# Attention of layer 1: the upper half copy of a slot's keys goes from VectorE to ScalarE

## The chip, the cores and the metric

The kernel runs on one core of one Trainium2 chip. The metric is the time of one execution on the device in microseconds, as the median of several runs.

## What is computed

The network has two layers, each an attention block and a feed-forward block, with a layer norm ahead of each and a residual behind it. The input is 16 sequences of 512 tokens with 256 features. Here only the attention block of layer 1 matters:

```python
h = _layernorm(x, ln1_g, ln1_b)
q, k, v = heads(h @ WQ + bQ), heads(h @ WK + bK), heads(h @ WV + bV)   # 16 heads of 16
scores = einsum('bhqd,bhkd->bhqk', q, k) / sqrt(16)
allowed = (diff >= 0) & (diff < 128)                   # each token sees the last 128
attn = softmax(where(allowed, scores, -inf))
attn_out = (attn @ v) @ WO + bO
u = h @ Bw;  s = A * s + u_t (scan over tokens);  ssm_out = states @ Cw
g = sigmoid(h @ Wg + bg)
x1 = x + g * attn_out + (1.0 - g) * ssm_out
return x1 + gelu(_layernorm(x1) @ W1 + b1) @ W2 + b2   # the MLP, 1024 wide
```

## The kernel before

The program is four phases, one after the other: attention 0 (names a_), a mixture of experts (b_), attention 1 (c_, `attn1_phase`), and a second mixture (d_). Each engine has its own instruction list, and semaphores tie the lists together. What is told here is of `attn1_phase`.

**One sequence at a time.** Each engine runs a `body(it)` for the 16 sequences, written out one after the other. In a body stand first the attention steps of sequence it, then, interleaved, the output part and the MLP of sequence it and the projections of sequence it+1. So the MLP of one sequence and the preparation of the next share the engines, in an order that is written out by hand. The profile's queues hold to that order: an instruction that waits holds up all that stand behind it on its engine.

**Slots.** The 16 heads go in 8 pairs, called slots here (j = 0 to 7). Queries and keys are projected in a packed form. `spread_qk` (TensorE, L2021) multiplies them by a table that lays the two heads of a slot out over 128 partitions: the first head on partitions 0 to 63, the second on 64 to 127. It has four matmuls a slot, two for the queries into one PSUM bank and two for the keys into another, each 128x512. Then the copies: ScalarE's `q4_copy` (L1638) takes the queries' bank to SBUF as a whole. VectorE's `k4_copy` takes the keys' bank to SBUF in two half copies of 64x512: the lower half (L1818) into `k4[0:64, j, 0]`, the upper half (L1819) into `k4[64:128, j, 1]`. The other quarters of `k4` are zeros, so that one matmul gives the scores of both heads. The semaphore `k4_ready` goes up once a slot.

**Banks.** Slots 0 to 2 (HELD = 3) use the banks `o_ps` for the queries and `c_ps` for the keys, slots 3 to 7 the two banks of `ab_ps`. There is one bank for queries and one for keys, so the matmuls of slot j wait until slot j−1 is copied: the queries' for `q4_ready`, the keys' for `k4_ready`.

**Where the slots stand.** Slots 0 to 2 of the next sequence stand in the MLP of this one: slot 0 before the first block of `mlp1`, slot 1 after its second block, slot 2 before the last block of `mlp2`. Slot 3 opens the body, and slots 4 to 7 follow the scores of steps 0 to 3.

**Steps.** 32 steps a sequence (n = 0 to 31): four blocks of 128 queries, eight slots each. A step is: scores on TensorE (`scores`, L2047 and L2048, into one of two banks `s_ps`), their maxima on VectorE (`maxima`, L1839), exponentials with their sums on ScalarE (`exp`, L1658, two a step), reciprocals of the sums on VectorE (L1844), the product on GpSimd (`normalise`, L1575), transposes on TensorE three steps later (`transposes`, L2060), their copy on ScalarE (`pT_copy`, L1669), and the product with the values on TensorE five steps later (L2080). On ScalarE each of the steps 0 to 3 has the `q4_copy` of slot n+4 ahead of its exponentials. On VectorE each of these steps has the maxima, then `k4_copy` of slot n+4, then the reciprocals of step n−1. The scores of step n wait for the exponentials of step n−2. At step 6 VectorE scales the gate (L1859), for which GpSimd's bias products wait, which stand ahead of the normalisation of step 5 there.

**MLP.** Eight blocks m: `mlp1` (TensorE, six matmuls of 128x512 into a bank of `ab_ps`), GELU on ScalarE (L1693), its high half on ScalarE (L1699), its low half on VectorE (L1880), then `mlp2` (TensorE, twelve matmuls of 128x256 into `s_ps`). TensorE runs mlp2(m), mlp1(m+2), mlp2(m+1), and so on. On ScalarE the query copy of slot 0 stands ahead of GELU of block 0, that of slot 1 behind the high half of block 0, and that of slot 2 behind all blocks, ahead of the table load for the exponentials (L1753). VectorE's `k4_copy` of slot 0 stands ahead of the low half of block 0, that of slot 1 behind it, and that of slot 2 behind the low half of block 7, ahead of the results (L1886).

Of the kernel before, what the change touches and what calls it, by code (L numbers as in the profile page):

```python
# [13 lines left out]
P = 128  # L14
# [537 lines left out]
def after(eng, sem, value):  # L552

    if not (isinstance(value, int) and value <= 0):
        eng.wait_ge(sem, value)
# [739 lines left out]
PAIRS1 = H1 // 2  # L1295
# [10 lines left out]
def attn1_phase(nc, x, out, wqk_d, wvg_d, bw_d, cw_d, wo_d, w1_d, w2_d, spread_d, cols_d, rows_d, b1_d, a_d, window_d, half_d, ident_d):  # L1306
# [7 lines left out]
    with ExitStack() as ctx:  # L1314
# [6 lines left out]
        def sem(nm):  # L1321
            return ctx.enter_context(nc.semaphore(f"c_{nm}"))
# [49 lines left out]
        a = sb("a", [P, 1])  # L1372
# [20 lines left out]
        k4 = sb("k4", [P, PAIRS1, 2, SEQ], F32R)  # L1393
# [35 lines left out]
        HELD = 3  # L1429
        q4_ps = [o_ps[:] if j < HELD else ab_ps[:, 0] for j in range(PAIRS1)]  # L1430
        k4_ps = [c_ps[:].rearrange("p a d -> p (a d)") if j < HELD else ab_ps[:, 1] for j in range(PAIRS1)]
# [16 lines left out]
        q4_ready = sem("q4_ready")  # L1448
        k4_in_psum = sem("k4_in_psum")
        k4_ready = sem("k4_ready")  # L1450
        vg_in_psum = sem("vg_in_psum")
        vg_ready = sem("vg_ready")
        gate_ready = sem("gate_ready")
# [164 lines left out]
        def _(act):  # L1618
# [16 lines left out]
            def q4_copy(it, j):  # L1635
                act.wait_ge(q4_in_psum, it * PAIRS1 + j + 1)
                after(act, s_ready, it * NS)
                nc.scalar.copy(q4[:, j], q4_ps[j]).then_inc(q4_ready, 1)  # L1638

            def gates(it):  # L1640

# [116 lines left out]
        def _(dve):  # L1758
# [56 lines left out]
            def k4_copy(it, j):  # L1815
                dve.wait_ge(k4_in_psum, it * PAIRS1 + j + 1)
                after(dve, s_ready, it * NS)
                nc.vector.tensor_copy(k4[0:P // 2, j, 0], k4_ps[j][0:P // 2])  # L1818
                nc.vector.tensor_copy(k4[P // 2:P, j, 1], k4_ps[j][P // 2:P]).then_inc(k4_ready, 1)  # L1819

            def scan(it):

# [146 lines left out]
        def _(pe):  # L1969
# [11 lines left out]
            def h_transposes(it, c):  # L1981

                if c == 0:
                    pe.wait_ge(hn_ready, it + 1)
                    after(pe, k4_ready, it * PAIRS1)
                else:
                    pe.wait_ge(hT_ready, it * DC + c)
                transpose_chunk(hn, ab_ps[:, 1], c).then_inc(hT_in_psum, 1)
# [17 lines left out]
            def spread_qk(it, j):  # L2006


                c, jj = divmod(j, PAIRS1 // 2)
                if j == 0:  # L2010

                    pe.wait_ge(qlo_ready, (it + 1) * 2 * DC)
                if j == HELD:
                    after(pe, ff_ready, it * MF)
                for a, (bank, full, free) in enumerate(((q4_ps[j], q4_in_psum, q4_ready), (k4_ps[j], k4_in_psum, k4_ready))):
                    if j:
                        pe.wait_ge(free, it * PAIRS1 + j)
                    elif a:
                        pe.wait_ge(state_ready, it + 1)
                    for half_ in range(2):  # L2020
                        last = nc.tensor.matmul(bank, spread[:, jj, 2 * a + half_], qk_hl[a][half_][:, c], start=(half_ == 0), stop=(half_ == 1))  # L2021
                    last.then_inc(full, 1)
# [12 lines left out]
            def scores(it, n):  # L2035
                i, j = divmod(n, PAIRS1)
                G = it * NS + n
                if n < PAIRS1:
                    pe.wait_ge(q4_ready, it * PAIRS1 + n + 1)
                    pe.wait_ge(k4_ready, it * PAIRS1 + n + 1)  # L2040
                if n == 0 and not first_step(it):
                    pe.wait_ge(result_ready, it * T - T // 2)
                elif n == 1:
                    after(pe, result_ready, it * T)
                after(pe, exp_ready, G - 1)
                keys_ = slice(max(i - 1, 0) * P, (i + 1) * P)
                nc.tensor.matmul(s_ps[:, n % 2, :, keys_of(i)], identb[:], maskb[:, :, keys_of(i)], start=True, stop=False, skip_group_check=True)  # L2047
                last = nc.tensor.matmul(s_ps[:, n % 2, :, keys_of(i)], q4[:, j, i * P:(i + 1) * P], k4[:, j, :, keys_], start=False, stop=True, skip_group_check=True)  # L2048
                last.then_inc(s_ready, 1)
# [33 lines left out]
            def mix(it, t):  # L2083

                pe.wait_ge(aolo_ready, it * T + t + 1)
                if t:
                    pe.wait_ge(mix_copied, it * T + t)
                else:
                    pe.wait_ge(statelo_ready, it + 1)
                    pe.wait_ge(k4_ready, it * PAIRS1 + HELD)  # L2090
                tok = slice(t * P, (t + 1) * P)

                nc.tensor.matmul(c_ps[:, 0], state_hl[:, tok], cw[0][:], start=True, stop=False)
                nc.tensor.matmul(c_ps[:, 0], state_hl[0:STATE, tok], cw[1][0:STATE], start=False, stop=True)
                for c in range(OC):
                    last = three(nc, c_ps[:, 1], [h[:, c] for h in aoT_hl], [w[:, c] for w in wo], c == 0, c == OC - 1)
                last.then_inc(mix_in_psum, 1)
# [703 lines left out]
```

## Time and profile before

| | us |
|---|---|
| median of 3 runs | 4868.71 (4868.36 to 4870.63) |
| the profiled execution, device time | 4830.12 |
| its span in the trace | 4828.2 |
| TensorE busy (matmuls) | 4069.7 (84%) |
| VectorE busy | 3098.1 (64%) |
| ScalarE busy | 2455.8 (51%) |
| GpSimd busy | 2304.5 (48%) |

The mean granted clock of TensorE is 0.95 of full speed. The trace numbers its times in microseconds from the start of the span. The attention of layer 1 fills roughly the stretch from 2710 to 4550 us, about 113 us a sequence. Names in the rows have their digits left out: `c_k` is `k4` (or `k`), `c_q` is `q4` (or another buffer that shares its place), `c_w` is `w1` or `w2`, `c_t` is `t1` or `t_ps`, `c_o_ps`, `c_c_ps`, `c_ab_ps` and `c_s_ps` are PSUM banks. L72 to L74 are the three matmuls of the helper `three`.

### The profile page before, as it was taken

The numbers are of one execution on the slowest core, as the hardware profiler recorded it, in microseconds if no ns is written. First come the engines' busy times: TensorE is split into PE (matmuls) and PEld (weight loads), VectorE is DVE, ScalarE is ACT, GpSimd is POOL, SyncE is SP. The second block draws the span as 40 slices with busy tenths as digits, with TensorE's granted clock in tenths as the row PEclk, the third lists the DMA queues.
The fourth block names the chain that finished last, engine by engine and source line by source line (L and its number), as shares of the span: only waits on it lengthen the run. The fifth ranks groups of instructions, "written<-read, shape, count | busy, mean of one in ns | idle before, by whom it ended". The sixth has DMA issues, their size and how long they took to land. (4 is left out here: it accounts for less than half of the span.)

```text
span 4828.2 us, 147864 instructions
## 1 busy us (share of the span) xinstructions
PE 4069.7 (84%) x60532; PEld 3223.2 (67%) x60628; DVE 3098.1 (64%) x7362; ACT 2455.8 (51%) x5553; POOL 2304.5 (48%) x2383
## 2 busy tenths in 40 slices
PE   3888888888888986888888589999999988999669
PEld 2676777677667775777777366666666666666568
DVE  3777777767677775677767555555555555555357
ACT  3555555555454542333323366666666666666436
POOL 4666566666665640000000355555555555555365
PEclk8999999999999998999999799999999999999759
DMA  2222222221222111000000100000000000000134
GB/s 84 54 49 60 63 48 51 65 60 47 51 69 50 46 43 49 27 18 26 18 27 13 61 10 10 10 10 10 10 10 10 10 18 10 10 10 6 62 133 139
DMA packets 152814, 188.09 MB, mean 39 GB/s; under 512 B 28254, under 2 KB 113377, under 8 KB 150753
## 3 DMA queue, kind: packets, MB, share of 16 engines
q1 hardware_dynamic: 145680, 162.05, 12.4%
q0 software_dynamic: 6480, 16.92, 1.0%
q8 instruction: 461, 7.55, 0.7%
q14 instruction: 193, 1.57, 0.1%
HBM read 68.48 MB, written 44.19 MB: 23 GB/s over the span
## 5 line engine op out<-in xcount | busy, mean ns | idle before, releaser
L1575 POOL TENSOR_TENSOR c_prob<-c_prob,c_inv 128x512 f32<-128x512 f32 (+1 forms) x512 | 477.3, 946 | 608.7 <-DVE c_inv L1844 599.1
L1658 ACT ACTIVATE c_prob<-c_s_ps,c_nmax 128x256 f32<-128x256 f32 (+1 forms) x1024 | 457.8, 462 | 228.7 <-DVE c_nmax L1839 226.7
L1839 DVE TENSOR_REDUCE c_nmax<-c_s_ps 128x2 f32<-128x512 f32 (+1 forms) x512 | 316.9, 620 | 272.6 <-PE c_s_ps L2048 268.3
L848 POOL TENSOR_TENSOR a_swap<-a_swap,a_sin 128x512 f32<-128x512 f32 x128 | 201.1, 1571 | 542.1 <-DMA a_swap<-a_raw 542.1
L2060 PE MATMUL c_t_ps<-c_ident,c_prob 128*128 128x128 f32 x1792 | 289.7, 278 | 76.5 <-POOL c_prob L1575 71.3
L212 POOL TENSOR_TENSOR b_var<-b_mv,b_eps 128x4 f32<-128x4 f32 x16 | 8.5, 532 | 693.0 <-DVE b_mv L304 692.9
L2060 PEld LDWEIGHTS c_t_ps<-c_ident,c_prob 128*128 128x128 f32 x1792 | 207.4, 141 | 177.8 <-POOL c_prob L1575 127.6
L889 ACT COPY a_raw<-a_w_ps 128x512 f32<-128x512 f32 x256 | 150.1, 586 | 339.8 <-PE a_w_ps L74 339.5
L1669 ACT COPY c_pT<-c_t_ps 128x512 f32<-128x512 f32 (+1 forms) x512 | 281.4, 550 | 57.2 <-PE c_ab_ps L2080 48.7
L1170 PE MATMUL a_w_ps<-a_mem,a_sT 64*32 64x65 f32 x14848 | 217.4, 226 | 95.9 <-issue 92.4
L2048 PE MATMUL c_s_ps<-c_k,c_q 128*128 128x512 f32 (+1 forms) x512 | 271.5, 530 | 5.2 <-ACT c_prob L1658 5.2
L252 ACT ACTIVATE b_s_sb<-b_gu_ps 128x512 f32<-128x512 f32 x144 | 86.1, 598 | 364.2 <-PE b_gu_ps L74 364.2
L1170 PEld LDWEIGHTS a_w_ps<-a_mem,a_sT 64*32 64x32 f32 x14848 | 171.3, 106 | 147.3 <-issue 125.2
L72 PE MATMUL b_y_ps<-b_wd_hi,b_h_hi 128*128 128x256 f32 x576 | 175.0, 304 | 94.0 <-DVE b_acc L406 47.0
L72 PE MATMUL a_w_ps<-a_xT_hi,a_wqk_hi 128*128 128x512 f32 x512 | 235.4, 460 | 21.0 <-DVE a_x_ln L968 13.3
L72 PE MATMUL b_gu_ps<-b_xT_hi,b_wgu_hi 128*128 128x512 f32 x576 | 233.4, 405 | 10.7 <-DVE b_xT_lo L373 10.7
L1880 DVE TENSOR_TENSOR c_hT_lo<-c_ff,c_hT_hi 128x512 fp32r<-128x512 f32 x128 | 88.5, 692 | 227.2 <-ACT c_hT_hi L1699 226.7
L73 PE MATMUL b_gu_ps<-b_xT_hi,b_wgu_lo 128*128 128x512 f32 x576 | 232.3, 403 | 0.0
L74 PE MATMUL b_gu_ps<-b_xT_lo,b_wgu_hi 128*128 128x512 f32 x576 | 229.5, 399 | 0.0
L1658 ACT ACTIVATION_READ_ACCUMULATOR c_prob<-c_s_ps,c_nmax 128x1 f32 x1024 | 221.8, 217 | 0.0
L73 PE MATMUL a_w_ps<-a_xT_hi,a_wqk_lo 128*128 128x512 f32 x512 | 218.7, 427 | 3.3 <-issue 3.3
L74 PE MATMUL a_w_ps<-a_xT_lo,a_wqk_hi 128*128 128x512 f32 x512 | 218.7, 427 | 2.5 <-issue 2.5
(405 smaller groups left out, 13686.5 us busy)
## 6 DMA issues: line engine op xcount, KB each, us to landing
a_swap<-a_raw SPq DMA_DIRECT2D x1024, 64.0 KB
d_xb<-sorted_rows SPq DMA_DIRECT2D x71, 130.0 KB
a_x_ln<-x SPq DMA_DIRECT2D x128, 64.0 KB, 2.1
a_acc<-x SPq DMA_DIRECT2D x64, 128.0 KB
after_attn<-a_acc SPq DMA_DIRECT2D x64, 128.0 KB, 2.4
b_x_in<-after_attn SPq DMA_DIRECT2D x16, 512.0 KB, 4.5
after_ffn<-b_acc SPq DMA_DIRECT2D x16, 512.0 KB, 3.2
c_x_in<-after_ffn SPq DMA_DIRECT2D x16, 512.0 KB, 4.6
```

What stands on the lines that cost most here:

```text
L72: nc.tensor.matmul(out, w[0], x[0], start=start, stop=False, **options)
L73: nc.tensor.matmul(out, w[1], x[0], start=False, stop=False, **options)
L74: return nc.tensor.matmul(out, w[0], x[1], start=False, stop=stop, **options)
L848: nc.gpsimd.tensor_tensor(q_sw, q_sw, table(sin), ALU.mult)
L889: (rawq_ready, rawk_ready)[a].by(nc.scalar.copy(raw[:, m % 3, a], bank))
L1170: ins = nc.tensor.matmul(into[s * SEG:(s + 1) * SEG, r, j], sT[d, (n // T * T + j) % (2 * PU), a, tok], mem[d, s, j], start=True, stop=True)
L1575: nc.gpsimd.tensor_tensor(p, p, inv[:, n % 4].unsqueeze(2).to_broadcast([P, 2, KB])[:, :, keys_of(i)], ALU.mult).then_inc(norm_ready, 1)
L1658: last = nc.scalar.activation(prob[:, n % 4, h, keys_of(i)], s_ps[:, n % 2, h, keys_of(i)], ACT.Exp, bias=nmax[:, n % 4, h:h + 1], accum_o ...
L1669: nc.scalar.copy(pT[:, n % 2, :, b[0]:2], t_ps[:, n % 2, :, b[0]:2]).then_inc(pT_ready, 1)
L1839: nc.vector.tensor_reduce(nmax[:, n % 4], s_ps[:, n % 2, :, keys_of(i)], AX.X, ALU.max, negate=True).then_inc(max_ready, 1)
L2048: last = nc.tensor.matmul(s_ps[:, n % 2, :, keys_of(i)], q4[:, j, i * P:(i + 1) * P], k4[:, j, :, keys_], start=False, stop=True, skip_gro ...
L2060: last = nc.tensor.transpose(t_ps[:, n % 2, h, b], prob[:, n % 4, h, b * P:(b + 1) * P], ident[:])
```

## The change

The lower half copy stays on VectorE and signals `k4_ready` by itself. The upper one goes to ScalarE, behind the query copy of the same slot, where it waits for the keys' matmuls and for the lower copy of its slot; it signals a new semaphore, `k4_upper`. All that waited on TensorE for `k4_ready` waits for `k4_upper`.

```diff
             def q4_copy(it, j):
                 act.wait_ge(q4_in_psum, it * PAIRS1 + j + 1)
                 after(act, s_ready, it * NS)
                 nc.scalar.copy(q4[:, j], q4_ps[j]).then_inc(q4_ready, 1)
+                act.wait_ge(k4_in_psum, it * PAIRS1 + j + 1)
+                act.wait_ge(k4_ready, it * PAIRS1 + j + 1)
+                nc.scalar.copy(k4[P // 2:P, j, 1], k4_ps[j][P // 2:P]).then_inc(k4_upper, 1)
...
             def k4_copy(it, j):
                 dve.wait_ge(k4_in_psum, it * PAIRS1 + j + 1)
                 after(dve, s_ready, it * NS)
-                nc.vector.tensor_copy(k4[0:P // 2, j, 0], k4_ps[j][0:P // 2])
-                nc.vector.tensor_copy(k4[P // 2:P, j, 1], k4_ps[j][P // 2:P]).then_inc(k4_ready, 1)
+                nc.vector.tensor_copy(k4[0:P // 2, j, 0], k4_ps[j][0:P // 2]).then_inc(k4_ready, 1)
...
                 if c == 0:
                     pe.wait_ge(hn_ready, it + 1)
-                    after(pe, k4_ready, it * PAIRS1)
+                    after(pe, k4_upper, it * PAIRS1)
...
-                for a, (bank, full, free) in enumerate(((q4_ps[j], q4_in_psum, q4_ready), (k4_ps[j], k4_in_psum, k4_ready))):
+                for a, (bank, full, free) in enumerate(((q4_ps[j], q4_in_psum, q4_ready), (k4_ps[j], k4_in_psum, k4_upper))):
...
                 if n < PAIRS1:
                     pe.wait_ge(q4_ready, it * PAIRS1 + n + 1)
-                    pe.wait_ge(k4_ready, it * PAIRS1 + n + 1)
+                    pe.wait_ge(k4_upper, it * PAIRS1 + n + 1)
...
                     pe.wait_ge(statelo_ready, it + 1)
-                    pe.wait_ge(k4_ready, it * PAIRS1 + HELD)
+                    pe.wait_ge(k4_upper, it * PAIRS1 + HELD)
```

## Rows read from the trace of the kernel before

**Rows 1.** The page's part 1: busy time, share of the span, instructions.

```profile
PE 4069.7 (84%) x60532; PEld 3223.2 (67%) x60628; DVE 3098.1 (64%) x7362; ACT 2455.8 (51%) x5553; POOL 2304.5 (48%) x2383
```

**Rows 2.** Windows, about one sequence: length, PE, PEld, DVE, ACT, POOL busy, clock, DMA.

```profile
3298.00:3411.40 113.40, 101.65 (x697) 73.61 (x704) 66.33 (x147) 72.17 (x207) 63.54 (x77) 1.00 0.04 12
```

**Rows 3.** Line L2021, TensorE's matmuls alone: idle us before them until, times.

```profile
  DVE c_k L1819: 52.5, 67
```

**Rows 4.** Line L1819: duration ns min/median/max, first and last start us.

```profile
L1819 DVE CAST c_k<-c_ab_ps x80: 694/695/695, 2733.3 to 4434.2; 64x512 fp32r<-64x512 f32 x80
```

**Rows 5.** Line L1638, the query copy, the same columns.

```profile
L1638 ACT CAST c_q<-c_ab_ps x80: 568/585/588, 2731.0 to 4432.0; 128x512 fp32r<-128x512 f32 x80
```

**Rows 6.** Timeline, head: start us, length us, engine, line, operation, idle before <-releaser.

```profile
3413.33 0.50 PE L2021 MATMUL c_ab_ps<-c_k_hi,c_spread 128*128 128x512 f32 x1 [0.78 <-DVE c_k L1819]
...
3413.67 0.39 PE L2021 MATMUL c_ab_ps<-c_k_lo,c_spread 128*128 128x512 f32 x1
...
3414.10 0.68 DVE L1818 CAST c_k<-c_ab_ps 64x512 fp32r<-64x512 f32 x1 [0.37 <-PE c_ab_ps L2021]
...
3414.80 0.69 DVE L1819 CAST c_k<-c_ab_ps 64x512 fp32r<-64x512 f32 x1
...
3415.54 0.50 PE L2021 MATMUL c_ab_ps<-c_k_hi,c_spread 128*128 128x512 f32 x1 [0.79 <-DVE c_k L1819]
```

**Rows 7.** Timeline, the start of the head.

```profile
3406.85 0.68 DVE L1818 CAST c_k<-c_c_ps 64x512 fp32r<-64x512 f32 x1 [0.27 <-PE c_c_ps L2021]
...
3406.99 1.28 ACT L1753 ACT_TABLE_LOAD   x1
...
3408.28 0.20 ACT L1753 ACTIVATE c_table<-c_b 128x1 f32<-128x1 f32 x1
...
3409.68 0.67 DVE L1818 CAST c_k<-c_ab_ps 64x512 fp32r<-64x512 f32 x1
...
3411.11 0.50 PE L2021 MATMUL c_ab_ps<-c_k_hi,c_spread 128*128 128x512 f32 x1 [0.90 <-DVE c_k L1819]
```

**Rows 8.** Timeline, the end of the head and the steps behind it.

```profile
3417.76 0.50 PE L2021 MATMUL c_ab_ps<-c_k_hi,c_spread 128*128 128x512 f32 x1 [0.79 <-DVE c_k L1819]
...
3418.39 0.37 ACT L1658 ACTIVATE c_prob<-c_s_ps,c_nmax 128x128 f32<-128x128 f32 x1 [0.80 <-DVE c_nmax L1839]
...
3420.60 0.37 ACT L1658 ACTIVATE c_prob<-c_s_ps,c_nmax 128x128 f32<-128x128 f32 x1 [1.14 <-DVE c_nmax L1839]
...
3420.86 0.44 PE L2060 MATMUL c_t_ps<-c_ident,c_prob 128*128 128x128 f32 x2 [1.13 <-POOL c_prob L1575]
...
3421.55 0.39 ACT L1658 ACTIVATE c_prob<-c_s_ps,c_nmax 128x128 f32<-128x128 f32 x1
...
3422.41 0.17 DVE L1844 RECIPROCAL c_inv<-c_psum 128x2 f32<-128x2 f32 x1
3422.49 0.67 DVE L1859 TENSOR_SCALAR c_gate<-c_gate 128x1024 f32<-128x1024 f32 x1
```

**Rows 9.** Timeline, slots 0 and 1 in the MLP.

```profile
3498.04 0.67 DVE L1818 CAST c_k<-c_c_ps 64x512 fp32r<-64x512 f32 x1
...
3499.20 0.69 ACT L1693 ACTIVATE c_ff<-c_ab_ps,c_b 128x512 f32<-128x512 f32 x1 [1.96 <-PE c_ab_ps L74]
...
3501.07 0.58 ACT L1638 CAST c_q<-c_o_ps 128x512 fp32r<-128x512 f32 x1 [0.52 <-PE c_o_ps L2021]
...
3501.53 0.68 DVE L1818 CAST c_k<-c_c_ps 64x512 fp32r<-64x512 f32 x1 [0.26 <-PE c_c_ps L2021]
3501.55 0.69 ACT L1693 ACTIVATE c_ff<-c_ab_ps,c_b 128x512 f32<-128x512 f32 x1
...
3502.27 0.62 ACT L1699 CAST c_hT_hi<-c_ff 128x512 fp32r<-128x512 f32 x1
...
3502.96 0.69 DVE L1880 TENSOR_TENSOR c_hT_lo<-c_ff,c_hT_hi 128x512 fp32r<-128x512 f32 x1
...
3504.23 0.28 PE L72 MATMUL c_s_ps<-c_w_hi,c_hT_hi 128*128 128x256 f32 x1
```

More of the change, by code:

```diff
@@ L1450, in attn1_phase @@
         k4_ready = sem("k4_ready")
+        k4_upper = sem("k4_upper")
         vg_in_psum = sem("vg_in_psum")
```

## The prediction

> **What bounds the kernel now.** I read three views: the busy times, the windows of the layer that is changed, then the order of time inside one sequence. Over the whole span TensorE is busy 84% and no other engine above 64% [rows 1]. One sequence of this layer takes about 113 us, and in such a window TensorE is busy 101.7 us, ScalarE 72.2 and VectorE 66.3 at a granted clock of 1.00 (2.4 GHz) [rows 2]. So a moved copy counts only where TensorE stands still and something waits for that copy. There is one such place: before the matmuls that spread the keys (L2021) TensorE stood idle 52.5 us until the upper half copy L1819 was done, 67 times [rows 3]. That is 0.78 us each and some four a sequence. The key bank of a slot is single from slot 3 on, so the chain goes round: key matmuls, lower copy, upper copy, key matmuls. From one pair of key matmuls to the next it takes 3415.54 − 3413.33 = 2.21 us [rows 6]. The matmuls end 0.73 us after they start, a hand-over takes 0.04 to 0.05, the lower copy 0.68 and the upper one 0.69 with 0.02 ahead of it. I call this run of slots the head of a sequence (slots 3 to 7, with the scores of steps 0 to 3 between them).
>
> In the MLP that follows, TensorE runs without a gap: the matmuls of the second layer's block 1 start at 3504.23, 0.58 us after the low half that they need was ready (3502.96 + 0.69 = 3503.65) [rows 9]. That 0.58 is all the cover that ScalarE's and VectorE's work has there.
>
> **The change, part by part.** 1. VectorE loses 128 upper copies of 0.695 us [rows 4]. Only those in the head are waited for.
>
> 2. ScalarE gains 128 copies of 64x512 from PSUM. The trace has no ScalarE instruction on 64 partitions. Its nearest row is the query copy of the same width, same types and same banks on 128 partitions, 0.585 us [rows 5]. The bound above is the removed copy itself, 0.695 [rows 4]; VectorE's lower half takes 0.68 [rows 6], so its upper partitions are dearer by some 0.01. Below, nothing in the trace shows fewer partitions to be cheaper, and I take 0.50 as the low end from the 0.48 us after which the next instruction followed a query copy (3501.55 − 3501.07) [rows 9]. I take 0.585.
>
> 3. The two halves don't run side by side. ScalarE waits for the lower half (k4_ready) before it starts the upper one, and TensorE now waits for k4_upper. So one slot goes 0.73 + 0.04 + 0.68 + 0.04 + 0.585 + 0.05 = 2.13; against the measured 2.21 I take the difference of the changed terms, 0.70 out (3414.10 + 0.68 to the end of L1819 is 0.71) and 0.63 in, and get 2.14: 0.07 saved a slot.
>
> 4. The start of the head. The upper copy of slot 2 falls between the query copy and the table load. Its lower half ends at 3406.85 + 0.68 = 3407.53, so the upper one ends at 3408.16 and the table load, 3406.99 before, starts at about 3408.18 and its probe ends at about 3409.7 [rows 7]. The query copy of slot 3 follows until about 3410.2. The lower copy of slot 3 starts at 3409.68 as now (it stands behind the results on VectorE) and ends at 3410.36, so ScalarE is free in time; its upper copy runs 3410.40 to 3410.99 and TensorE goes on at 3411.04 where it did at 3411.11 [rows 7]. So the table load's cover is 0.2 us wide, and the start gives 0.07.
>
> 5. What is queued behind the wait on ScalarE. Exponentials of step n now stand behind the upper copy of slot n+4. The key matmuls of slot 7 start at 3417.76 now [rows 8], and 0.07 + 3 × 0.07 = 0.28 earlier after: 3417.48. Then 0.73 + 0.04 + 0.68 + 0.04 + 0.585 brings the upper copy's end to 3419.56, and the exponentials of step 3 start at about 3419.46 (0.10 before that end, as 3501.55 stands against 3501.65 in rows 9). Now they start at 3418.39. They are 1.07 us late, but ScalarE has had a hole until 3420.60 there: the step's exponentials and copy take 0.70 and 0.25 (3420.60 to 3421.55 is 0.95) [rows 8]. So step 4 starts at 3419.46 + 0.95 = 3420.41 and step 5 at 3421.36, where they start at 3420.60 and 3421.55 now: 0.19 earlier. The transposes of step 2, which wait for GpSimd at 3420.86 (idle 1.13), then wait for ScalarE's copy of step 0 instead, at about 3420.5. Step 5 is what the gate's scaling at 3422.49 waits for, and through GpSimd the transposes of step 5. I carry 0.19 us a sequence to the end: 16 × 0.19 = 3.0 us gained.
>
> 6. The MLP. The upper copy of slot 1 comes between the query copy and the GELU of block 1. Its lower half runs 3501.53 to 3502.21, so ScalarE stands until 3502.25 where GELU ran from 3501.55 [rows 9]. GELU then starts at 3502.25 + 0.585 − 0.10 = 3502.74, its high half 0.72 later at 3503.46, the low half on VectorE at 3503.46 + 0.62 + 0.04 = 3504.12, which ends 0.69 later at 3504.81, and TensorE goes on at 3504.86 instead of 3504.23: 0.63 us lost. The next blocks have their 0.58 of cover again and lose nothing more, but nothing gives the 0.63 back, since TensorE is without gaps up to the head. This happens in 15 sequences (the last has no successor): 15 × 0.63 = 9.4 us lost. The copies of slot 0 and slot 2 are covered: slot 0's upper half would end at 3499.35 and GELU of block 0 begins at 3499.25 instead of 3499.20 [rows 9], which the later wait swallows; slot 2's is point 4.
>
> 7. The two waits that ScalarE gains a slot: no row prices them alone. A hand-over with its wait takes 0.04 to 0.05 [rows 6] and stands in the sum already; a second wait costs between nought, if it is met by then, and another 0.05. I take nought, since the key matmuls that it names are done before the lower copy starts. TensorE's waits change their name only. VectorE's earlier maxima and reciprocals in the head: nothing on the path, since step 3 onward goes by ScalarE.
>
> Sum: −3.0 + 9.4 = +6.4 us. The profiled execution took 4830.1 us (span 4828.2), 38.6 under the median of 4868.7; the sum shifts both alike: 4836.5 and, as the prediction, 4875.1.
>
> **The rivals.** *No overlap behind a half copy.* ScalarE starts the next instruction 0.10 us before a 128-partition copy ends. If behind one that covers 64 partitions it waits for the end, GELU and step 3's exponentials come 0.10 later. For it: VectorE's upper copy, which begins on other partitions than the instruction ahead, starts 0.02 after that one's end (3414.78, 3414.80) [rows 6], while the gate's scaling starts 0.09 before the reciprocal ahead of it ends (3422.58, 3422.49) [rows 8]. Against it: no row of ScalarE shows this. Price 15 × 0.73 − 16 × 0.09 = +9.5: 4878.2.
>
> The Trainium skill (VectorE: DVE Perf Modes, Two Vector instructions with no wait between them) has a VectorE instruction held until the earlier ones are done if its input or output starts in another quarter of the partitions. VectorE's rows agree; of ScalarE it states nothing. If it held there too the sum would be this rival's.
>
> *A dearer upper copy (the slower side).* If it takes 0.695 us on ScalarE, the MLP wait is 0.63 + 0.11 = 0.74, and five copies in the head's chain cost 5 × 0.11 more: −0.19 + 0.55 = +0.36. 15 × 0.74 + 16 × 0.36 = +16.9: 4885.6. It decides from 0.62 us on: each 0.01 costs 0.95 us in the whole, and 0.035 carry the sum over the bound of 0.2%. The query row speaks against it, the dearer upper half on VectorE a little for it.
>
> *ScalarE becomes the limit.* It is the busier of the two, 72.2 against 66.3 us in a window [rows 2]. If all 128 copies landed on the path, 128 × 0.585 = +74.9: 4943.6. Its 41 us of idle time a sequence speak against it.
>
> The Trainium skill (Perfetto Trace Analysis, Optimizing Scalar/DVE Operations) has work moved to ScalarE when VectorE is saturated; by that rule this move goes the wrong way, from the emptier to the fuller engine, and the rows agree that neither is saturated.
>
> *The MLP wait is swallowed.* If VectorE or TensorE has more cover than the 0.58 us, only the head's gain is left: −3.0, 4865.7.
>
> *More comes back in the head (faster).* If the gap of 1.13 us ahead of step 2's transposes [rows 8] closed and the whole of it reached the end, 16 × 1.13 = 18.1 gained against 9.4: −8.7, 4860.0, and with the copies at 0.50 us another 8: 4852. ScalarE's queue of point 5 speaks against it.
>
> **How the numbers follow.** A measurement of this kernel can tell a change from none at about 0.2%, 9.7 us. Forecast +6.4: 0.40. No overlap +9.5: 0.18, half on each side of the bound. Dearer copy: 0.23. ScalarE the limit: 0.02. MLP wait swallowed: 0.08. More in the head: 0.09. So faster 0.09, same 0.40 + 0.09 + 0.08 = 0.57, slower 0.09 + 0.23 + 0.02 = 0.34. The range leaves out the far halves of the last rivals: 4862 to 4887.
>
> **What would show it.** The upper copy on ScalarE in a row of its own: 0.585 us, or not. The step between key matmuls 2.14. Idle time of the keys' matmuls ended by ScalarE, about 0.9 us a slot in the head. Before the second layer's block 1 a gap of 0.6 us, 15 times, ended by VectorE's low half. Exponentials of step 3 about 1.07 us later and of step 5 about 0.19 earlier, against the start of the head. Wrong I would be if the copy's price is not the query copy's, or if the 1.07 us late exponentials reach TensorE before the hole at step 4 takes them in.

## The result and the profile after

| | before | after |
|---|---|---|
| time, median of 6 runs each | 4868.53 us | 4891.38 us |
| spread of the runs | 4863.76 to 4871.19 | 4884.21 to 4898.98 |
| ratio, 95% interval | | 1.0049 [1.0037, 1.0062] |
| profiled execution | 4830.1 (span 4828.2) | 4898.0 (span 4896.2) |
| layer-1 attention, key matmuls of slot 3, first to last sequence | 1692.2 | 1713.4 |

The change makes the kernel slower by 0.49% (22.9 us between the medians), where I had forecast 6.4 us and a range up to 4887. The two profiled spans differ by 68 us, which is no measure of the change: the profiled execution of before lay 38 us under its median, and only 21.2 us of the 68 lie in the stretch that is changed. That 21.2 is of one execution each; it is near the timed 22.9, and it is what I take apart below. An undisturbed sequence is one in which TensorE's clock stays at full speed. From one sequence's key matmuls of slot 3 to the next one's it took 112.62 us before and takes 113.70 now (medians of the 13 and the 9 such sequences behind the first): 1.08 more, where I expected 0.63 − 0.19 = 0.44. The median of all 15 sequences of after is 113.85.

The profile of after, part 1 of the page (busy time, share of the span, instructions):

```profile
PE 4118.3 (84%) x60532; PEld 3239.6 (66%) x60628; DVE 3001.6 (61%) x7234; ACT 2528.1 (52%) x5681; POOL 2311.0 (47%) x2383
```

128 instructions have moved from VectorE to ScalarE, as the change says [rows 1]. The moved copy has a row of its own, L1642, with the columns of rows 4:

```profile
L1642 ACT CAST c_k<-c_ab_ps x80: 581/581/582, 2753.0 to 4473.8; 64x512 fp32r<-64x512 f32 x80
```

0.581 us against the 0.585 that I took. The two windows of after beside rows 2, one undisturbed sequence and one that isn't:

```profile
2866.07:2979.76 113.69, 102.93 (x697) 73.44 (x702) 59.50 (x138) 76.38 (x215) 63.88 (x77) 1.00 0.03 10
2979.76:3094.90 115.14, 105.28 (x698) 74.49 (x702) 59.54 (x138) 76.56 (x215) 63.92 (x77) 0.97 0.03 10
```

VectorE lost 6.8 us a sequence and ScalarE gained 4.2; neither is near the window's length. Idle time ahead of the spreading matmuls and their weight loads (rows 3 has the matmuls alone), until the upper copy was done, before (L2021) and after (L2024):

```profile
  DVE c_k L1819: 135.0, 134
...
  ACT c_k L1642: 61.0, 85
```

These waits are now ended by ScalarE, and they are shorter. Others grew.

The waits in the layer-1 attention of after (waiting engine, what it writes, line, releaser: us in total, times, longest). The first line was 21.7 us in 60 times before, and the second 7.8 us in 30:

```profile
PE c_s_ps L2050 <- ACT c_prob L1662: 48.6, 90, 1.6
PEld c_s_ps L72 <- DVE c_hT_lo L1883: 24.2, 45, 1.1
```

Both are waits for work that is merely queued behind the moved copy: the exponentials in the head and the GELU in the MLP. Here is slot 1 in the MLP of after, timeline, with the columns of rows 6:

```profile
3414.35 0.40 PE L2024 MATMUL c_o_ps<-c_q_hi,c_spread 128*128 128x512 f32 x1
...
3415.01 0.59 ACT L1639 CAST c_q<-c_o_ps 128x512 fp32r<-128x512 f32 x1 [0.33 <-PE c_o_ps L2024]
...
3415.48 0.68 DVE L1822 CAST c_k<-c_c_ps 64x512 fp32r<-64x512 f32 x1
...
3416.25 0.58 ACT L1642 CAST c_k<-c_c_ps 64x512 fp32r<-64x512 f32 x1 [0.65 <-DVE c_k L1822]
...
3416.86 0.69 ACT L1697 ACTIVATE c_ff<-c_ab_ps,c_b 128x512 f32<-128x512 f32 x1
...
3417.58 0.62 ACT L1703 CAST c_hT_hi<-c_ff 128x512 fp32r<-128x512 f32 x1
...
3418.23 0.69 DVE L1883 TENSOR_TENSOR c_hT_lo<-c_ff,c_hT_hi 128x512 fp32r<-128x512 f32 x1 [2.07 <-ACT c_hT_hi L1703]
...
3418.98 0.39 PE L72 MATMUL c_s_ps<-c_w_hi,c_hT_hi 128*128 128x256 f32 x1 [0.45 <-DVE c_hT_lo L1883]
```

ScalarE stands 0.65 us for the lower half, with the GELU of block 1 behind it. GELU starts 3416.86 − 3415.01 = 1.85 us after the start of the query copy, where it started 3501.55 − 3501.07 = 0.48 after [rows 9]. TensorE then stands 0.45 us before the second layer's block 1, where it had no gap. The head of the next sequence:

```profile
3442.02 0.50 PE L2024 MATMUL c_ab_ps<-c_k_hi,c_spread 128*128 128x512 f32 x1 [0.73 <-ACT c_k L1642]
...
3446.36 0.50 PE L2024 MATMUL c_ab_ps<-c_k_hi,c_spread 128*128 128x512 f32 x1
...
3447.91 0.58 ACT L1642 CAST c_k<-c_ab_ps 64x512 fp32r<-64x512 f32 x1 [0.29 <-DVE c_k L1822]
...
3448.51 0.37 ACT L1662 ACTIVATE c_prob<-c_s_ps,c_nmax 128x128 f32<-128x128 f32 x1
...
3449.46 0.27 PE L2050 MATMUL c_s_ps<-c_maskb,c_identb 128*128 128x256 bf16 x1 [1.57 <-ACT c_prob L1662]
3449.47 0.39 ACT L1662 ACTIVATE c_prob<-c_s_ps,c_nmax 128x128 f32<-128x128 f32 x1
...
3450.41 0.41 ACT L1662 ACTIVATE c_prob<-c_s_ps,c_nmax 128x128 f32<-128x128 f32 x1
...
3451.38 0.68 DVE L1862 TENSOR_SCALAR c_gate<-c_gate 128x1024 f32<-128x1024 f32 x1
```

The exponentials of step 3 start 2.15 us after slot 7's key matmuls (3446.36 to 3448.51) where they started 0.63 after [rows 8]. TensorE stands 1.57 us for them at 3449.46, before the scores of step 5; before the change it stood 0.19 us there (3419.34), and then 1.13 us for GpSimd at the next transposes [rows 8]. The gate's scaling comes 5.02 after slot 7's key matmuls, 4.73 before.

### The profile page after: what moved, and what is told of

Read it like the earlier page. It is cut to its first block and busy times, and to the rows that moved or that the text cites. A ratio compares the mean times of both kernels' runs of the same rounds, so it can differ in the third digit from the quotient of the medians.

```text
span 4896.2 us, 147992 instructions
## 1 busy us (share of the span) xinstructions
PE 4118.3 (84%) x60532; PEld 3239.6 (66%) x60628; DVE 3001.6 (61%) x7234; ACT 2528.1 (52%) x5681; POOL 2311.0 (47%) x2383
```

## The experiments

Below, a sequence is split at the same instructions in each kernel: the start of the key matmuls of slot n (k3, k4, k7), the gate's scaling, and the start of the query matmuls of the MLP's slots 0 to 2 (q0, q1, q2). All are medians over the sequences of one profiled execution, in us, and right to 0.01; the whole sequence is the median of the undisturbed ones behind the first. The ratios against the kernel before are of timed runs, with their 95% interval; each is taken against runs of before on the same chip, e1 and e2 on one, e5 to e9 on a second, e10 to e12 on a third. e3 and e4 were run once each (4865.80 and 4874.73 us, before beside them 4857.67), so they have no ratio.

| kernel | k3→k4 | k4→k7 | k7→gate | gate→q0 | q1→q2 | sequence | ratio |
|---|---|---|---|---|---|---|---|
| before | 2.50 | 6.65 | 4.74 | 72.19 | 19.23 | 112.62 | 1 |
| after | 2.47 | 6.52 | 5.02 | 72.27 | 20.15 | 113.70 | 1.0049 [1.0037, 1.0062] |
| e1_head_scalar | 2.46 | 6.52 | 5.01 | 72.20 | 19.23 | 112.72 | 1.0016 [1.0001, 1.0031] |
| e2_mlp_scalar | 2.51 | 6.65 | 4.75 | 72.26 | 20.15 | 113.58 | 1.0034 [1.0017, 1.0052] |
| e3_one_wait | 2.41 | 6.36 | 4.96 | 72.26 | 20.08 | 113.37 | |
| e4_swapped | 2.60 | 6.56 | 5.34 | 72.19 | 20.02 | 113.58 | |
| e5_parallel | 1.89 | 5.20 | 4.74 | 72.21 | 19.51 | 110.83 | 0.9928 [0.9910, 0.9945] |
| e6_slot1_later | 2.47 | 6.53 | 5.01 | 72.22 | 19.44 | 112.95 | 1.0002 [0.9992, 1.0011] |
| e8_exp_first | 2.41 | 6.36 | 4.26 | 72.23 | 19.38 | 111.92 | 0.9972 [0.9960, 0.9984] |
| e9_parallel_exp_first | 1.89 | 5.82 | 4.07 | 72.26 | 19.23 | 110.54 | 0.9922 [0.9908, 0.9935] |
| e10_last_exp_first | 1.88 | 5.21 | 4.76 | 72.18 | 19.23 | 110.57 | 0.9920 [0.9901, 0.9939] |
| e11_last_exp_first_swapped | 2.03 | 4.76 | 4.26 | 72.27 | 19.23 | 109.83 | 0.9904 [0.9885, 0.9924] |
| e12_changed_again | 2.47 | 6.53 | 5.02 | 72.28 | 20.15 | 113.73 | 1.0037 [1.0023, 1.0051] |

### The change in two parts

e1 leaves the copies of slots 0 to 2, those in the MLP, on VectorE; e2 does the opposite (`if j < HELD:` in both places).

```diff
+                if j >= HELD:
                     act.wait_ge(k4_in_psum, it * PAIRS1 + j + 1)
-                    act.wait_ge(k4_ready, it * PAIRS1 + j + 1)
+                    act.wait_ge(k4_ready, it * (PAIRS1 - HELD) + j - HELD + 1)
                     nc.scalar.copy(k4[P // 2:P, j, 1], k4_ps[j][P // 2:P]).then_inc(k4_upper, 1)
...
-                nc.vector.tensor_copy(k4[0:P // 2, j, 0], k4_ps[j][0:P // 2]).then_inc(k4_ready, 1)
+                low = nc.vector.tensor_copy(k4[0:P // 2, j, 0], k4_ps[j][0:P // 2])
+                if j >= HELD:
+                    low.then_inc(k4_ready, 1)
+                else:
+                    nc.vector.tensor_copy(k4[P // 2:P, j, 1], k4_ps[j][P // 2:P]).then_inc(k4_upper, 1)
```

> Only slots 3 to 7 have their upper half copy on ScalarE; slots 0 to 2, in the MLP, are copied by VectorE as before the change. Theory Q (the loss comes from the place of the copy in ScalarE's queue): the stretch from slot 1's to slot 2's spreading matmuls falls back from 20.15 to 19.23 us, the head stays as changed (slot 4 to slot 7 6.52 us, slot 7 to the gate's scaling 5.02), so a sequence takes 112.8 us against 113.70 changed and 112.62 before, and the kernel is 2 to 4 us slower than before. Theory C (TensorE is granted its lower level more often, wherever the copies stand): some 10 us or more of the loss stay.

> The reverse: only slots 0 to 2 have their upper half copy on ScalarE. Theory Q: slot 1's to slot 2's matmuls 20.15 us as changed, slot 4 to 7 6.65 and slot 7 to the gate 4.74 as before, a sequence 113.54 us, the kernel 13 to 15 us slower than before (15 x 0.92). Theory C: the loss divides by the number of copies moved, three of eight, 9 us. A third, that slot 1's loss is given back in the head: under 5 us.

Measured: the head alone costs 0.16%, the MLP alone 0.34%, together 0.50% where the whole change costs 0.49%; the intervals are ±0.15 wide, so that the sum fits this closely is luck. In the traces the layer, first to last sequence, is 1.8 us longer than before in e1 (1694.0) and 18.2 in e2 (1710.4), against 21.2 in after. e1 has the MLP of before (19.23) with the head of after (5.01), and e2 the reverse. So the two effects add to within a microsecond or two, the MLP is the larger, and the head loses some 0.1 us a sequence, where I had it gain. e1's timed 8.6 us are more than the 2 to 4 expected and than the 1.5 that its sequences explain; the interval reaches down to 0.5 us, and no trace shows the rest.

### One wait less

```diff
-                act.wait_ge(k4_in_psum, it * PAIRS1 + j + 1)
                 act.wait_ge(k4_ready, it * PAIRS1 + j + 1)
                 nc.scalar.copy(k4[P // 2:P, j, 1], k4_ps[j][P // 2:P]).then_inc(k4_upper, 1)
```

> The changed kernel without ScalarE's wait for the keys' matmuls, which the wait for the lower half implies. It asks where the 0.09 to 0.10 us from the end of the lower half to the start of the upper one come from, where other hand-overs take 0.04. If from the second wait: 0.04 here, slot 4 to slot 7 6.52 - 3 x 0.05 = 6.37 us, slot 1's to slot 2's matmuls 20.10. If from ScalarE reading other partitions or from VectorE's late end of a PSUM copy: no difference from the changed kernel.

e3 ran once, so I read its trace alone. Slot 1 in the MLP of e3:

```profile
3394.60 0.68 DVE L1821 CAST c_k<-c_c_ps 64x512 fp32r<-64x512 f32 x1
...
3395.32 0.58 ACT L1641 CAST c_k<-c_c_ps 64x512 fp32r<-64x512 f32 x1 [0.60 <-DVE c_k L1821]
...
3395.93 0.69 ACT L1696 ACTIVATE c_ff<-c_ab_ps,c_b 128x512 f32<-128x512 f32 x1
```

From the end of the lower copy to the start of the upper it takes 3395.32 − 3395.28 = 0.04 us. In after it takes 3416.25 − 3416.16 = 0.09. The wait that I had put at nought, long met as it was, costs 0.05 a slot. Without it k4→k7 goes from 6.52 to 6.36, which is three slots of 0.05, and q1→q2 from 20.15 to 20.08. The whole head, k3 to the gate, takes 13.74, where it takes 14.01 in after and 13.89 before. So this one wait, five times in the head's chain, turns a gain of 0.15 us a sequence into a loss of 0.12.

### The halves swapped

```diff
-                nc.scalar.copy(k4[P // 2:P, j, 1], k4_ps[j][P // 2:P]).then_inc(k4_upper, 1)
+                nc.scalar.copy(k4[0:P // 2, j, 0], k4_ps[j][0:P // 2]).then_inc(k4_upper, 1)
...
-                nc.vector.tensor_copy(k4[0:P // 2, j, 0], k4_ps[j][0:P // 2]).then_inc(k4_ready, 1)
+                nc.vector.tensor_copy(k4[P // 2:P, j, 1], k4_ps[j][P // 2:P]).then_inc(k4_ready, 1)
```

> The changed kernel with the halves swapped: ScalarE copies the lower half (partitions 0 to 63) and VectorE the upper one (0.695 us for 0.683). It asks why the instruction behind the half copy on ScalarE starts 0.02 to 0.03 us after its end and not 0.10 before it. If other start partitions hold it up: here GELU of block 1 starts 0.10 before the copy's end, slot 1's to slot 2's matmuls take about 20.05 us instead of 20.15, and the exponentials of step 3 follow 0.10 closer. If 64 partitions alone do it: 20.15 to 20.17 stay.

Slot 1 in the MLP of e4:

```profile
3507.10 0.69 DVE L1822 CAST c_k<-c_c_ps 64x512 fp32r<-64x512 f32 x1
...
3507.88 0.58 ACT L1642 CAST c_k<-c_c_ps 64x512 fp32r<-64x512 f32 x1 [0.67 <-DVE c_k L1822]
...
3508.37 0.68 ACT L1697 ACTIVATE c_ff<-c_ab_ps,c_b 128x512 f32<-128x512 f32 x1
```

ScalarE's copy lasts the same 0.58, but now GELU starts at 3508.37, 0.09 before the copy's end at 3508.46. In after it starts at 3416.86, 0.03 behind the end at 3416.83. Behind none of the 128 half copies of after does the next instruction start before the copy's end (0.02 us behind it at the earliest); in e4 the median is 0.10 before it. So my rival *no overlap* was true of this change, and what goes with it is that the copy begins at partition 64 and the instruction behind it at 0. ScalarE holds here as the Trainium skill (VectorE: DVE Perf Modes, Two Vector instructions with no wait between them) says of VectorE. In time the swap brings little here: q1→q2 goes to 20.02 and, where TensorE's clock kept up, k7→gate to 4.87, 0.15 under after, but k3→k7 is 0.17 longer (9.16 against 8.99). In 12 of the heads behind the first the clock of TensorE was lower for a while (part 8 below), which puts the median of k7→gate at 5.34. A single execution can't tell what the lower clock has to do with the swap.

### Side by side

ScalarE doesn't wait for VectorE's half any more; TensorE waits for both halves wherever it waited for the upper one.

```diff
                 act.wait_ge(k4_in_psum, it * PAIRS1 + j + 1)
-                act.wait_ge(k4_ready, it * PAIRS1 + j + 1)
                 nc.scalar.copy(k4[P // 2:P, j, 1], k4_ps[j][P // 2:P]).then_inc(k4_upper, 1)
...
+                    pe.wait_ge(k4_ready, it * PAIRS1 + n + 1)
                     pe.wait_ge(k4_upper, it * PAIRS1 + n + 1)
```

> The changed kernel, but ScalarE no longer waits for the lower half, so the two halves of a slot run side by side on the two engines; TensorE waits for both. The queue order stays. Theory Q: the head's chain loses a copy and ScalarE's own work (query copy 0.59, half copy 0.60, exponentials 0.70) sets the pace: slot 4 to slot 7 about 5.7 us instead of 6.52, slot 7 to the gate 4.25 instead of 5.02; slot 1's GELU is 0.73 instead of 1.36 us late, so slot 1's to slot 2's matmuls 19.5. A sequence 111.5 us, 15 to 20 us faster than before. Rival: two engines on one PSUM bank slow each other (copies above 0.62 and 0.70 us) and nothing is gained over the changed kernel. Theory C: no better than the changed kernel.

A slot in the head of e5:

```profile
3309.00 0.68 DVE L1821 CAST c_k<-c_ab_ps 64x512 fp32r<-64x512 f32 x1 [0.67 <-PE c_ab_ps L2026]
...
3309.51 0.58 ACT L1641 CAST c_k<-c_ab_ps 64x512 fp32r<-64x512 f32 x1
...
3310.11 0.37 ACT L1661 ACTIVATE c_prob<-c_s_ps,c_nmax 128x128 f32<-128x128 f32 x1
3310.14 0.50 PE L2026 MATMUL c_ab_ps<-c_k_hi,c_spread 128*128 128x512 f32 x1
```

Both engines read the same bank for a while, and each takes its usual 0.68 and 0.58. ScalarE's copy starts 0.51 behind VectorE's because ScalarE was busy until then: it sets the pace, 5.20 / 3 = 1.73 us a slot against 2.17. k7→gate goes back to 4.74, as the exponentials still stand behind the copy, but the copy no longer waits. From k4 to the gate it is 9.94, as expected (5.7 + 4.25), though split otherwise. The kernel is 0.72% faster than before, more than the 15 to 20 us expected: the half copy on the other engine is worth something, and what cost was its wait for the first half.

### The same copies at another place in the queue

e6 takes one instruction of the changed kernel, the upper copy of slot 1, and puts it behind the high half of block 1 (L1703), so that GELU 1 doesn't stand behind its wait.

```diff
+            def k4_upper_copy(it, j):
                 act.wait_ge(k4_in_psum, it * PAIRS1 + j + 1)
                 act.wait_ge(k4_ready, it * PAIRS1 + j + 1)
                 nc.scalar.copy(k4[P // 2:P, j, 1], k4_ps[j][P // 2:P]).then_inc(k4_upper, 1)
...
                     ff_hi(it, m)
+                    if not last_step(it) and m == 1:
+                        k4_upper_copy(it + 1, 1)
```

> The changed kernel with one move in ScalarE's list: slot 1's upper half copy stands behind the high half of block 1 instead of ahead of GELU of block 1. All 128 copies stay on ScalarE. Theory Q: slot 1's to slot 2's matmuls 20.15 -> 19.23 us, a sequence 112.78 us, 2 to 4 us slower than before and 14 faster than changed. Theory C or a price of the copies themselves: no change against the changed kernel, some 20 us slower than before.

q1→q2 falls from 20.15 to 19.44, the gap before block 1 of the second layer is in no sequence, and the loss of the whole kernel is gone within the interval: 1.0002 [0.9992, 1.0011]. The work on each engine is the same as in after. That leaves 0.21 over the 19.23 of before. It comes from the upper copy of slot 0, which stands in the same way ahead of the GELU of block 0. Timeline of e6:

```profile
3380.51 0.58 ACT L1646 CAST c_k<-c_c_ps 64x512 fp32r<-64x512 f32 x1 [1.53 <-DVE c_k L1830]
...
3381.12 0.69 ACT L1701 ACTIVATE c_ff<-c_ab_ps,c_b 128x512 f32<-128x512 f32 x1
...
3383.24 0.39 PE L72 MATMUL c_s_ps<-c_w_hi,c_hT_hi 128*128 128x256 f32 x1
```

GELU follows the copy, and the second layer's block 0 starts 1.12 us after slot 1's query matmuls (3382.12) instead of 0.93. I had put the delay of this GELU at 0.05; with the second wait (0.05) and the lost overlap (0.10) on top it is 0.19 in after (GELU starts 1.01 instead of 1.20 ahead of slot 1's query matmuls). In after the later wait for block 1 covers it. With one wait less (e8) block 0 starts at 1.06, and at 0.93 where nothing on ScalarE waits for VectorE's half (e5, e9, e10, e11).

e8 takes e6, leaves the second wait out and puts the upper copies of slots 4 to 7 behind the exponentials of steps 0 to 3.

```diff
                     exp(it, n)
+                    if HELD + 1 + n < PAIRS1:
+                        k4_upper_copy(it, HELD + 1 + n)
```

> As the one with slot 1's copy later, with one wait less, and in the head each step's exponentials ahead of the half copy instead of behind it; the halves still one after the other. Theory Q: the exponentials fit in ScalarE's hole of 0.28 us and more before the half copy, slot 4 to slot 7 stays at 6.36 us as with one wait, slot 7 to the gate falls from 5.02 to about 4.3 (before: 4.74), a sequence 111.8 us, 10 to 13 us faster than before. Rival: the half copy now comes late for the next key matmuls and slot 4 to 7 grows over 6.65: same as before or slower.

k7→gate falls to 4.26, under the 4.74 of before, while k4→k7 stays at the 6.36 of e3. Against e3, which differs in the order and in slot 1's place, k7→gate is 0.70 shorter. ScalarE would have stood there for VectorE anyway, so the exponentials cost nothing ahead of the copy. This kernel has serial halves and all upper copies on ScalarE, and is faster than before by 0.28%. So the moved copies by themselves, or ScalarE's load, are not the loss.

### Which order, when the halves run side by side

e9 is e5 with the places of e8; e10 puts only slot 7's upper copy behind the exponentials of its step (`if n == 3`); e11 is e10 with the halves swapped as in e4.

> Both: halves side by side, slot 1's copy behind block 1, exponentials ahead of the half copies in the head. Theory Q: slot 4 to slot 7 5.7 us, slot 7 to the gate 3.8 to 4.2, slot 1's to slot 2's matmuls 19.23, a sequence 110.7 to 111.2 us, 20 to 32 us faster than before. Rival: the exponentials hold the half copies up and the head is no shorter than with the plain order (then no faster than the parallel one).

> Halves side by side, slot 1's upper copy behind block 1, and in the head the plain order for slots 4 to 6 but the exponentials of step 3 ahead of slot 7's half copy. Theory Q, from the measured parts: slot 4 to 7 5.21 us as in the parallel kernel, slot 7 to the gate 4.07 to 4.3 as with exponentials first, slot 1's to slot 2's matmuls 19.23. A sequence 110.0 to 110.2 us, 38 to 42 us faster than before. Rival: the two orders trade the same 0.6 us, slot 4 to the gate stays at 9.9: a sequence 110.55 as in the kernel with all exponentials first, 36 us faster.

> The same with the halves swapped: ScalarE takes partitions 0 to 63, VectorE 64 to 127. ScalarE's instruction behind the half copy then starts 0.10 us before its end, VectorE's own starts are held up instead. If ScalarE's queue sets the pace of the head (1.74 us a slot in the parallel kernel): 0.2 us less a slot, slot 4 to 7 4.7 to 4.9 us, a further 4 to 6 us faster. If the loop of key matmuls, VectorE's copy and hand-overs sets it: no difference or 0.02 us a slot more.

e9 gives 5.82 + 4.07 = 9.89 from k4 to the gate, e10 5.21 + 4.76 = 9.97, e5 5.20 + 4.74 = 9.94: the order only shifts 0.6 us from one side of slot 7 to the other, and what I had called the rival for e10 came true. The 0.26 us a sequence that e10 has over e5 is slot 1's copy in the MLP (19.23 against 19.51), not the order in the head. Behind slot 7 of e10 TensorE waits for ScalarE at the step 5 scores and again at the transposes, timeline of e10:

```profile
3287.51 0.58 ACT L1645 CAST c_k<-c_ab_ps 64x512 fp32r<-64x512 f32 x1
...
3287.63 0.27 PE L2063 MATMUL c_s_ps<-c_maskb,c_identb 128*128 128x256 bf16 x1 [0.57 <-ACT c_prob L1665]
...
3288.12 0.37 ACT L1676 COPY c_pT<-c_t_ps 128x256 f32<-128x256 f32 x1
...
3288.63 0.41 PE L2076 MATMUL c_t_ps<-c_ident,c_prob 128*128 128x128 f32 x2 [0.61 <-ACT c_pT L1676]
```

Once ScalarE sets the pace, whatever takes time off ScalarE counts. That is what e11 shows: with its copies on partitions 0 to 63 the next instruction overlaps again, timeline of e11:

```profile
3290.00 0.58 ACT L1639 CAST c_q<-c_ab_ps 128x512 fp32r<-128x512 f32 x1
...
3290.36 0.69 DVE L1831 CAST c_k<-c_ab_ps 64x512 fp32r<-64x512 f32 x1 [0.24 <-PE c_ab_ps L2036]
3290.47 0.60 ACT L1645 CAST c_k<-c_ab_ps 64x512 fp32r<-64x512 f32 x1
...
3290.95 0.39 ACT L1665 ACTIVATE c_prob<-c_s_ps,c_nmax 128x128 f32<-128x128 f32 x1
```

The exponential starts 0.12 before the copy ends at 3291.07, and the half copy itself starts 0.11 before the query copy ahead of it ends (3290.58), where in e10 it starts 0.02 behind that end (3282.95 and 3282.97). So each slot gets back some 0.2 us: k4→k7 is 4.76, and a sequence takes 109.83 instead of 110.57. e11 has the lowest ratio of all, 0.9904, almost 1% under before; its interval overlaps that of e10, so that the swap is worth something is shown by the traces (first to last sequence 1650.8 against 1660.5 us) and not by the times.

### The changed kernel once more

e12 is the changed kernel without any edit.

> The changed kernel once more, beside these on one chip. Theory Q: 16 to 23 us slower than before, a sequence without a fall of the clock 113.70 us. If lower clock after long stalls of TensorE adds to it, a few sequences stand 0.3 to 1.4 us above that, more than in the kernels whose head is shorter (those show none).

1.0037 [1.0023, 1.0051], 17.0 us between the medians, and the same medians to 0.01 us in the head and the MLP (6.53, 5.02, 20.15). What differs between its trace and that of after is TensorE's clock. It was under full speed in the head of nine sequences behind the first, of five in after and of one in before.

## Why the prediction missed the size

The direction of the middle value held, and so did the copy's price and the MLP wait at the place I named. The size didn't: 21.2 us in the layer instead of 6.4. Two terms of the sum failed: the second wait on ScalarE, which I took at nought and which costs 0.05 us each time (step 7), and the overlap of 0.10 behind a half copy, which isn't there (the rival *no overlap*). Together they turned the head's gain of 3.0 us into a loss (step 5) and made the MLP's term too small (step 6). Step by step, with the numbers of the prediction:

1 and 2. Right. The upper copy takes 0.581 on ScalarE, forecast 0.585. The rival *a dearer copy*, 0.695, fell, though it came nearest in its total (16.9).

3. The slot. k4→k7 is 6.52 / 3 = 2.17 us, not 2.14: 0.04 saved, not 0.07. The terms were right but for the hand-over of 0.09 where I had 0.04.

4. Start of the head. 0.03 gained instead of 0.07, the same 0.05. In the first sequence it went worse: the upper copy of slot 2 stands ahead of the first gate activation and the table load, whose cover isn't there, and TensorE waited 1.52 us for a query copy. Timeline of after, first sequence:

```profile
2749.17 0.58 ACT L1642 CAST c_k<-c_c_ps 64x512 fp32r<-64x512 f32 x1 [1.47 <-DVE c_k L1822]
2749.78 1.06 ACT L1647 ACTIVATE c_gate<-c_gate 128x1024 f32<-128x1024 f32 x1
...
2753.00 0.80 PE L2024 MATMUL c_ab_ps<-c_q_hi,c_spread 128*128 128x512 f32 x1 [1.52 <-ACT c_q L1639]
```

That sequence took 116.26 us against 114.20, 2.06 more, some 1.0 over the common 1.08. I had read only the head of a sequence in the middle.

5. The head's end: the step whose sign failed. ScalarE's queue went as I had it: behind the late exponentials of step 3 those of steps 4 and 5 follow without idle time, 0.96 and 0.94 us apart (forecast 0.95 each). But the exponentials of step 3 start 2.15 us behind slot 7's key matmuls, not 3419.46 − 3417.48 = 1.98: the second wait (0.05), the lost overlap (0.10) and 0.02 of rounding. The 0.17 reaches the exponentials of step 5, which start 4.05 after k7 instead of 3.88 (before: 3.79), and k7→gate lost 0.28 where I had 0.09. With −0.03 and −0.13 the head costs +0.12 a sequence, not −0.19. e3 shows which term flips the sign: without the second wait the head takes 13.74, 0.15 less than before. What I had written as the sign of being wrong was seen, too: the late exponentials reach TensorE, as the scores of step 5 wait 1.57 us for them, a wait that I had left out. It didn't hold ScalarE up, though: the maxima of those scores end at 3450.31 (3449.89 + 0.42), 0.10 ahead of the exponentials at 3450.41, for which ScalarE had no idle time. That the exponentials' place matters at all is shown by e8: with them ahead of the copy k7→gate is 4.26.

6. The MLP: right place, too small. The GELU of block 1 is 1.36 us later (2.51 after slot 1's query matmuls, 1.15 before) where I had 1.19, through the hand-over (0.05), the lost overlap (0.10) and 0.02 of rounding. The start of the second layer's block 1 comes 0.80 later against the query matmuls, not 0.63. And q1→q2 grew by 0.92: behind the new gap the second matmul starts 0.22 us after the first (3418.98), where the next ones, and those of before at the same place, are 0.12 apart. A gap isn't the only thing that goes with this: at block 0, behind the spreading matmuls and without a gap, the two are 0.22 apart before as well. After:

```profile
3419.20 0.28 PE L73 MATMUL c_s_ps<-c_w_hi,c_hT_lo 128*128 128x256 f32 x1
...
3419.32 0.28 PE L74 MATMUL c_s_ps<-c_w_lo,c_hT_hi 128*128 128x256 f32 x1
```

0.80 and 0.10 are 0.90 of the 0.92. So 15 × 0.92 = 13.8 us instead of 9.4. That slots 0 and 2 cost nothing was right in the sequences behind the first; for slot 0 it is so only since the wait at block 1 covers its 0.19, as e6 shows.

7. The second wait: wrong. Nought was the low end of my bounds and the wrong one to take; 0.05 a slot was the high end, and it is what e3 measured. In the head's chain it stands five times, 0.27 us a sequence.

8. Not in the sum at all: TensorE's granted clock. These are windows of 5 us at the same place in two sequences of after, the columns of rows 2. The first line of each pair begins 10 us after the key matmuls of slot 3:

```profile
2876.07:2881.07 5.00, 3.44 (x28) 2.00 (x29) 3.09 (x11) 4.70 (x22) 2.10 (x4) 1.00 0.00 2
2881.07:2886.07 5.00, 3.56 (x25) 1.79 (x24) 2.07 (x7) 3.37 (x15) 4.69 (x8) 1.00 0.02 5
...
2989.76:2994.76 5.00, 3.44 (x25) 2.08 (x25) 3.09 (x10) 4.69 (x22) 2.07 (x4) 0.90 0.00 0
2994.76:2999.76 5.00, 4.55 (x20) 1.94 (x20) 1.61 (x6) 2.60 (x11) 4.40 (x7) 0.50 0.00 0
```

In the second sequence the clock falls to 0.50 of full speed, 1.2 GHz, behind a stretch in which TensorE was busy 3.44 of 5 us, as it was in the first sequence, where the clock stayed at 2.4 GHz. It falls 14.0 us behind k3. From 60 us ahead of k3 up to there the 423 matmul records of the two sequences start within 0.02 us of each other, so that what the kernel did just before doesn't tell the two apart. Such a sequence takes 1.4 us longer (115.14 against 113.69); others lose less. Over the layer the sequences of after behind the first exceed the undisturbed 113.70 by 5.4 us, those of before their 112.62 by 1.3: some 4.0 us. A head with shorter stalls seems to be what matters: it happens in no sequence behind the first of e5, e8, e9 and e10, whose heads take 11.8 to 13.0 us from k3 to the gate, and in one of e11 (11.1); it happens with the heads of 13.7 to 14.0 us of e1, e2, e3, e6 and e12 in three to nine, and in twelve of e4. Before, with 13.9, has one. The number varies between two executions of one kernel (five and nine), so this is a correlation; no run here separates it from chance in a single kernel.

Sum: 15 × 1.08 = 16.2, the first sequence 1.0, the clock 4.0: the 21.2 of the layer. The three are cut out of that same 21.2, so that they add up is no proof. gate→q0 grew by 0.08, which is in the 1.08: some 0.06 of it in e2 and none in e1, but none in e10 either, which has the MLP's copies on ScalarE as well; the cause is open.

The range ended at 4887 since I priced each rival alone. The second wait and the lost overlap were true together and pushed the same way: in my own sum they add 0.15 to the 0.63 of the MLP and 0.35 to the −0.19 of the head, 15 × 0.78 + 16 × 0.16 = +14.3 us, 4883.0. The rest of the miss is what the sum had no term for: the clock, the first sequence, the wider spacing at block 1 and gate→q0.

## What to carry to other kernels

Before moving a piece of work to another engine, write down what stands behind its wait in that engine's list; the wait delays it as well as the piece. Here the copies of 0.58 us cost 0.5% in one order of the list and nothing that the interval shows with one of the eight of each sequence a few places later. They gained 0.7 to 0.8% once ScalarE no longer waited for VectorE's half, in any order, and almost 1% with the halves swapped as well. If the two halves don't depend on one another, let the reader wait for both, not the one half for the other.

A wait that has long been met is not free on an engine that sets the pace, and costs that push the same way belong in one case, not in a rival each.

## What the runs showed of the hardware

- A PSUM copy of 64 partitions by 512 takes as long on ScalarE as one of 128: 0.581 and 0.585 us (after, before).
- On ScalarE the instruction behind a copy that begins at partition 64, itself beginning at 0, starts 0.03 us after its end (after); behind one that begins at 0 it starts 0.09 to 0.12 before its end (e4, e11). The other way round it is the same: a half copy that begins at partition 64 starts 0.02 after the end of the query copy ahead (e10), one that begins at 0 starts 0.11 before it (e11).
- A second, already met wait ahead of a ScalarE copy adds 0.05 us (0.09 in after against 0.04 in e3).
- ScalarE and VectorE reading the two halves of one PSUM bank at the same time slow each other by nothing that the trace shows (0.58 and 0.68 us in e5, as in after).
- Behind a gap of 0.45 us the second matmul of TensorE started 0.22 us after the first instead of 0.12 (after); the same 0.22 stands in before without a gap, behind the spreading matmuls (3501.33 and 3501.55).
- TensorE's clock fell to 1.2 GHz in the head of some sequences and not of others, at the same busy time ahead of it (3.44 of 5 us, after) and with the same matmuls within 0.02 us for 60 us and more.
